# Normalized rows split into float16 halves before they are turned, and turned by DMA: a cross-attention and mixture-of-experts kernel

## What is computed

```
x = x + attention(layernorm(x), ctx)      # 16 heads of 128, 8 key/value groups, Wq Wk Wv Wo
x = x + ffn(layernorm(x))                 # the feed-forward part:
#   shared = silu(x @ shared_gate) * (x @ shared_up) @ shared_down
#   gate: sigmoid(x @ gate_w.T) + bias, best 2 of 4 groups, best 4 of 32 experts, weights normalized
#   each expert takes at most 128 rows: silu(rows @ w1) * (rows @ w3) @ w2, weighted, added to its rows
```

## Time and profile before

| | us |
|---|---|
| median of 3 runs (1817.03 to 1822.59) | 1819.76 |
| the profiled execution | 1819.97 |
| its span | 1817.9 |
| TensorE busy in the span | 1655.7 |
| VectorE busy | 1282.2 |
| ScalarE, GpSimd busy | 704.2, 650.9 |
| mean granted clock of TensorE | 0.975 |

### The profile page before, as it was taken

One profiled execution on the slowest core, in us unless ns is written; L12 is line 12 of the kernel. 1 busy time (PEld: TensorE's weight loads), 2 busy tenths in 40 slices (PEclk: granted clock), 3 DMA queues, 4 the chain that ended last, 5 costly groups with the idle time before them and its releaser, 6 DMA issues.

```text
span 1817.9 us, 32885 instructions
## 1 busy us (share of the span) xinstructions
PE 1655.7 (91%) x11472; PEld 1101.2 (61%) x11472; DVE 1282.2 (71%) x3690; ACT 704.2 (39%) x1866; POOL 650.9 (36%) x985
## 2 busy tenths in 40 slices
PE   4889999999999999999999999999999996767774
PEld 3556666666766676767676767676767673333332
DVE  5778686767676767777677777676767576676674
ACT  4454343434343434343334333333333332344452
POOL 1222333333333333333323232424242424554553
PEclk9999999999999999999999999999999998898898
DMA  6543333323233323332323232323232328699973
GB/s 187 148 120 72 59 77 59 77 59 77 59 77 55 76 57 71 58 75 59 77 53 83 53 83 53 83 53 81 55 74 51 72 51 278 185 282 263 260 213 47
DMA packets 343779, 180.63 MB, mean 99 GB/s; under 512 B 277824, under 2 KB 314688, under 8 KB 343616
## 3 DMA queue, kind: packets, MB, share of 16 engines
q1 hardware_dynamic: 332352, 161.66, 36.4%
q0 software_dynamic: 11264, 16.87, 4.6%
HBM read 85.58 MB, written 25.85 MB: 61 GB/s over the span
## 4 chain that ended last, share of the span: by engine, by line
PE 64%; DMA 12%; DVE 12%; issue 6%; ACT 3%; POOL 2%; POOLq 0%; SPq 0%; DVEq 0%; ACTq 0%
DMA out_rows_dram<-weight_in,table 9%; PE ps_out L1267 6%; PE ps_fill L1268 6%; PE ps_fill L1269 6%; PE ps_fill L1267 6%; PE ps_out L1269 6%; PE ps_out L1268 6%; PE ps_query L1267 4%; PE ps_query L1268 4%; PE ps_query L1269 4%; DVE arena L946 3%; PE ps_score L1267 3%; PE ps_score L1268 3%; PE ps_score L1269 3%; ACT arena L664 2%
## 5 line engine op out<-in xcount | busy, mean ns | idle before, releaser
L491 POOL TENSOR_SCALAR arena<-arena,prob_scale 128x256 f16<-128x256 f32 x512 | 264.3, 532 | 662.2 <-DVE prob_scale L940 662.2
L664 ACT ACTIVATE arena<-arena,neg_max 128x256 f32<-128x256 f32 x512 | 253.9, 497 | 552.7 <-DVE neg_max L931 552.7
L1267 PE MATMUL ps_query<-xn_t,arena 128*128 128x256 f16 x1024 | 279.8, 273 | 2.6 <-issue 1.5
L1268 PE MATMUL ps_query<-xn_t,arena 128*128 128x256 f16 x1024 | 279.8, 273 | 0.0
L1269 PE MATMUL ps_query<-xn_t,arena 128*128 128x256 f16 x1024 | 279.7, 273 | 0.0
L931 DVE CUSTOM_DVE_ANT_0 arena<-ps_score,mask_add 128x256 f32<-128x256 f32 x512 | 186.6, 420 | 112.0 <-PE ps_score L1269 111.1
L946 DVE SCALAR_TENSOR_TENSOR arena<-arena,prob_scale 128x256 f16<-128x256 f32 x512 | 260.1, 547 | 3.7 <-POOL arena L491 3.7
L1267 PE MATMUL ps_out<-arena,o_t 128*128 128x512 f16 x512 | 195.3, 381 | 33.3 <-DVE o_t L951 27.4
L1269 PE MATMUL ps_out<-arena,o_t 128*128 128x512 f16 x512 | 194.8, 380 | 0.0
L1268 PE MATMUL ps_out<-arena,o_t 128*128 128x512 f16 x512 | 194.8, 380 | 0.0
L855 DVE SCALAR_TENSOR_TENSOR k_t<-ps_fill,k_t 128x256 f16<-128x256 f32 x128 | 54.3, 425 | 173.4 <-ACT k_t L604 173.4
(11 more groups left out here) (198 smaller groups left out, 3827.4 us busy)
## 6 DMA issues: line engine op xcount, KB each, us to landing
arena<-w SPq DMA_DIRECT2D x96, 512.0 KB
x_in<-x SPq DMA_DIRECT2D x16, 512.0 KB, 3.9
xn_rows<-xn SPq DMA_DIRECT2D x16, 512.0 KB, 3.7
out_rows_dram<-x SPq DMA_DIRECT2D x32, 256.0 KB
ctx_in<-ctx_t SPq DMA_DIRECT2D x16, 256.0 KB, 3.6
weight_in<-wq SPq DMA_DIRECT2D x4, 1024.0 KB, 6.4
weight_in<-wo SPq DMA_DIRECT2D x4, 1024.0 KB, 5.9
arena<-arena SPq DMA_TRANSPOSE x128
```

What stands on the lines that cost most here:

```text
L491: pool.tensor_scalar(p_rows[:, 0, c, :], probs[:, c, :], prob_scale[:, c:c + 1], 1.0, ALU.mult, ALU.mult).then_inc(norm_hi, 1)
L664: act.activation(probs[:, c, :], probs[:, c, :], ACT.Exp, bias=neg_max[:, c:c + 1], scale=-1.0, accum_out=prob_sum[:, c:c + 1]).then_inc(e ...
L1267: pe.matmul(dst, a.hi, b.hi, start=start and n == 0, stop=False)
L1268: pe.matmul(dst, a.hi, b.lo, start=False, stop=False)
```

## The change

The normalized rows are split into halves as rows. xn_high (ScalarE) and xn_rest (VectorE) read the float32 rows and write xn_half, [row, half, feature] in float16; a DMA transpose on SP's queue (turn_xn) writes both halves of 128 rows, turned, into xn_both. For xn2 it is the same with xn2_high, xn2_rest and turn_xn2. The DMA transposes have half the size of turn_probs (128 x 1024 float16), two per batch for each of the two. TensorE's transposes of these rows go, but for the last batch's xn2, which TensorE turns in float16, eight tiles per 128 rows, and ScalarE copies. The value filler of turn 1's second place moves to turn 2's second place. xn2_half goes to DRAM as pairs of float16 halves, 2048 bytes per row as before; the experts' gathers read them, TensorE turns eight float16 tiles and ScalarE copies them at once, without splitting. store_xn2 moves from turn 1 to turn 2. The float32 rows get other places (x1 and parts of weight_in), expert_h moves to hidden.

```diff
+            def turn_xn(b, t):
+                if b >= 2:
+                    sp.wait_ge(pe_query, KV * (b - 1))
+                sp.wait_ge(xn_lo, TB * b + t + 1)
+                sp.dma_start_transpose(xn_both[b % 2][:, :, :, t * P:(t + 1) * P].rearrange("p h k c -> p (h k) c"),
+                                       xn_half[:, t, :, :].rearrange("p h d -> p (h d)")).then_inc(xt_turned, 16)
+
+            def turn_xn2(z, t):
+                if z:
+                    sp.wait_ge(pe_up, FSB * z)
+                sp.wait_ge(xn2_lo, TB * z + t + 1)
+                sp.dma_start_transpose(xn2_both[:, :, :, t * P:(t + 1) * P].rearrange("p h k c -> p (h k) c"),
+                                       xn2_half[:, t, :, :].rearrange("p h d -> p (h d)")).then_inc(x2t_turned, 16)
...
             sp.dma_start(bias_row[:, :], gate_bias.broadcast_to([P, E])).then_inc(in_const, 16)
+            for t in range(TB):
+                turn_xn(0, t)
             load_weight(2)
...
                 turn_probs(i)
-                if j == 1 and b:
+                if j == 2 and b:
+                    for t in range(TB):
+                        turn_xn2(b - 1, t)
                     store_xn2(b - 1)
+                if j in (4, 5) and b + 1 < B:
+                    turn_xn(b + 1, j - 4)
...
         def first(b, j):
             a, z = b + 1, b - 1
+            if j < 2:
+                return ("value", a, j, 0) if b and a < B else None
             if b == 0:
-                return ("xt", 1, j - 4) if j in (4, 5) else None
-            if j in (0, 1):
-                return ("value", a, j, 0) if a < B else None
-            if j in (4, 5):
-                return ("xt", a, j - 4) if a < B else None
-            return {2: ("x2t", z, 0), 3: ("gate", z), 6: ("rank", z), 7: ("down", z, 0)}[j]
+                return None
+            return {3: ("gate", z), 6: ("rank", z), 7: ("down", z, 0)}.get(j)
 
         def second(b, j):
...
-            if j in (0, 1):
-                return ("value", a, j, 1) if a < B else None
-            if j == 2:
-                return ("x2t", z, 1)
-            return ("up", z, j - 3) if j < 7 else ("down", z, 1)
+            if j in (0, 2):
+                return ("value", a, j // 2, 1) if a < B else None
+            return {1: None, 7: ("down", z, 1)}[j] if j in (1, 7) else ("up", z, j - 3)
...
+            def xn2_high(z, t):
+                act.wait_ge(x1_normed, TB * z + t + 1)
                 if z:
-                    act.wait_ge(pe_up, FSB * z)
-                turned_high(ps, xn2_t, t, pe_x2t, x2t_hi, TB * z + t + 1)
+                    act.wait_ge(x2t_turned, 16 * TB * z)
+                    act.wait_ge(out_xn2, 16 * z)
+                else:
+                    act.wait_ge(out_blank, 48)
+                act.activation(xn2_half[:, t, 0, :], xn2_full[:, t, :], ACT.Copy, scale=X_S).then_inc(xn2_hi, 1)
...
+                if j in (4, 5) and b + 1 < B:
+                    xn_high(b + 1, j - 4)
...
+                if j == 1 and b and i < TURNS:
+                    for t in range(TB):
+                        xn2_high(b - 1, t)
...
+            def xn2_rest(z, t):
+                dve.wait_ge(xn2_hi, TB * z + t + 1)
+                dve.scalar_tensor_tensor(xn2_half[:, t, 1, :], xn2_full[:, t, :], X_S, xn2_half[:, t, 0, :], ALU.mult,
+                                         ALU.subtract).then_inc(xn2_lo, 1)
...
+                if j == 2 and routed:
+                    xn2_rest(z, 0)
                 if live:
                     prob_scales(i)
                     filler(first(b, j), ps_fill[1])
+                if j in (4, 5) and live and a < B:
+                    xn_rest(a, j - 4)
...
+                if j == 2 and routed:
+                    xn2_rest(z, 1)
...
-            def rows_low(e):
...
             def query(i, h):
                 b, g = divmod(i, KV)
                 if h == 0:
-                    pe.wait_ge(xt_lo, TB * (b + 1))
+                    pe.wait_ge(xt_turned, 16 * TB * (b + 1))
...
+            def x2t_ready(z):
+                if z < B - 1:
+                    pe.wait_ge(x2t_turned, 16 * TB * (z + 1))
+                else:
+                    pe.wait_ge(last_copied, TB)
 
             def gate(ps, z):
-                pe.wait_ge(x2t_lo, TB * (z + 1))
+                x2t_ready(z)
...
-                rows = rows_in[e % 3].rearrange("c (p k) -> c k p", k=KD)
-                transposes(ps_fill[e % 2], [rows[:, k, :] for k in range(KD)], pe_rows)
+                rows = rows_in[e % 3].rearrange("c (h p k) -> c h k p", h=2, k=KD)
+                for n in range(2 * KD):
+                    m = pe.transpose(ps_turn[e % 2][:, n * P:(n + 1) * P], rows[:, n // KD, n % KD, :], ident_half)
+                m.then_inc(pe_rows, 1)
...
             z = B - 1
+            pe.wait_ge(ident_halved, 1)
             pe.wait_ge(*emptied(before["end", 1]))
-            xn2_transposed(ps_fill[1], z, 0)
+            last_transposed(0)
```

More of the change, by code:

```diff
@@ L118, in build @@
         x_in = [sbuf(f"x_in{n}", [TB, D]) for n in range(2)]
-        normed = sbuf("normed", [TB, D])
-        xn_t = [split(f"xn_t{n}", [KD, T]) for n in range(2)]
+        xn_half = sbuf("xn_half", [TB, 2, D], F16)
+        xn_both = [sbuf(f"xn_both{n}", [2, KD, T], F16) for n in range(2)]
+        xn_t = [Split(both[:, 0], both[:, 1]) for both in xn_both]
         ctx_in = sbuf("ctx_in", [KC, S])
@@ L146, in build, with xn_full @@
         x1 = sbuf("x1", [TB, D])
-        xn2 = sbuf("xn2", [TB, D])
-        xn2_t = split("xn2_t", [KD, T])
+        xn2_half = sbuf("xn2_half", [TB, 2, D], F16)
+        xn2_both = sbuf("xn2_both", [2, KD, T], F16)
+        xn2_t = Split(xn2_both[:, 0], xn2_both[:, 1])
+        spare = weight_in[0][:, :].rearrange("p (n t d) -> p n t d", n=2, t=TB)
+        xn2_full = spare[:, 1]
+        def xn_full(b):
+            return x1[:, :, :] if b < 2 else spare[:, 0]
         tanh_g = sbuf("tanh_g", [T])
@@ L187, in build @@
                     for n in range(AHEAD, AHEAD + HELD)]
-        rows_in = [x_in[0][:, 0, :], x_in[0][:, 1, :], x_in[1][:, 0, :]]
-        rows_t = xn_t
+        rows_in = [rows.bitcast(F16) for rows in (x_in[0][:, 0, :], x_in[0][:, 1, :], x_in[1][:, 0, :])]
+        rows_both = [both[:, :, :, :].rearrange("p h k t -> p (h k t)")[:, 0:2 * D].rearrange(
+            "p (h k c) -> p h k c", h=2, k=KD) for both in xn_both]
+        rows_t = [Split(both[:, 0], both[:, 1]) for both in rows_both]
         table = sbuf("table", [E, 2], U32)
         slot_weight = sbuf("slot_weight", [E])
-        expert_h = normed[:, 0, 0:F]
+        expert_h = hidden[:, :]
         expert_h_t = [h_t[:, 0:FB, 0:P], h_t[:, FB:2 * FB, 0:P]]
@@ L201, in build @@
         ps_any = ps_fill + ps_score
+        ps_turn = [ps[:, :].bitcast(F16) for ps in ps_fill]
         consts = signal("consts")
@@ L756, in act_program @@
                 expert_high(0, part)
-            x2t_high(ps_fill[1], z, 0)
-            x2t_high(ps_fill[0], z, 1)
+            for t in range(TB):
+                xn2_high(z, t)
+            for t in range(TB):
+                last_copy(t)
             gate_exp_neg(ps_fill[1], z)
@@ L1208, in dve_program @@
             x1_norm(z)
-            x2t_low(ps_fill[1], z, 0)
-            x2t_low(ps_fill[0], z, 1)
+            for t in range(TB):
+                xn2_rest(z, t)
             expert_low(0, 1)
@@ L1244, in dve_program @@
                 add_shared(ps_fill[t], z, t)
-            for e in range(2):
-                rows_low(e)
             for e in range(E + 1):
@@ L1293, in key @@
                 pe.wait_ge(weight_lo, prepared["wk"])
-                pe.wait_ge(*emptied(before["key", i]))
+                if i:
+                    pe.wait_ge(*emptied(before["key", i]))
                 products(ps_fill[0][:, 0:S], [(wk_s[:, k, g * HD:(g + 1) * HD], ctx_s[b % 2][:, k, :])
@@ L1302, in value, with last_transposed @@
                                     for k in range(KC)]).then_inc(pe_value, 1)
[L1304 to L1310 removed]
+            def last_transposed(t):
+                pe.wait_ge(xn2_lo, TB * (B - 1) + t + 1)
+                for n in range(2 * KD):
+                    h, k = divmod(n, KD)
+                    m = pe.transpose(ps_turn[1 - t][:, n * P:(n + 1) * P], xn2_half[:, t, h, k * P:(k + 1) * P], ident_half)
+                m.then_inc(pe_x2t, 1)
+            def x2t_ready(z):
[3 more added lines that the diff above has]
+                    pe.wait_ge(last_copied, TB)
             def gate(ps, z):
[L1313 removed]
+                x2t_ready(z)
                 pe.wait_ge(weight_lo, prepared["gate"])
@@ L1345, in filler @@
                     return
-                pe.wait_ge(*emptied(before[use]))
+                if use in before:
+                    pe.wait_ge(*emptied(before[use]))
                 kind, *at = use
@@ L1430, in pe_program @@
             pe.wait_ge(consts, CONSTS)
-            for t in range(TB):
-                x_t(ps_fill[t], 0, t)
```

140 lines of the change are left out of this document (56 added, 84 removed).

## The result

| | before | after |
|---|---|---|
| median, us | 1821.17 (4 runs, 1817.03 to 1823.10) | 1846.45 (4 runs, 1844.45 to 1849.55) |
| ratio, 95% interval | | 1.0143 [1.0119, 1.0168] |
| the profiled execution, its span | 1819.97, 1817.9 | 1849.55, 1847.8 |
| 14 batches, start of the second to start of the last | 1299.66 | 1327.51 |

Slower by 1.4%: +25 us in the medians where +14.6 was forecast, inside the range and on the forecast side. The two profiled executions are 29.9 us of span apart (the one of after is the longest of its four). By stage, from profile to profile: start to the first scores -1.9 (24.46 to 22.53), first batch +1.1, the fourteen batches +27.9, the last batch's turns +2.2, from there to the first gather -1.1, experts +1.8.

What follows compares the result with a forecast made beforehand. TensorE was taken to bound the fifteen batches behind the first. Batches +19.6, start -2, last batch's end -1.6, first batch -0.4, experts -1 sum to +14.6 us on the base: 1834.6 us, range 1818 to 1860.

Steps and rivals of the forecast that it cites:

- Rival 1: Whole kernel: the removed TensorE time counts and the gate doesn't wait, 1789 us; chance 0.11.
- rival 2: Turn 3: halves turn nearly at copy speed, gate waits 0.5 us, total 1812 to 1818; chance 0.14, spread over 1808 to 1826.
- rival 3: DMA transposes: each set-up of 1.81 us not overlapped adds 27 us (1862), two give 1889; chance 0.17 shared with two others.
- Rival 5: DMA transposes with a strided target split into smaller packets, looking like dearer turns; chance 0.17 shared with two others.
- Turn 1: Each batch: turn keeps its length since VectorE's o_t sets it; 1.64 us become idle for TensorE.
- Turn 2: Each batch: o_t starts later because xn2_rest precedes prob_scale; +0.5 us, between +0.2 and +0.6.
- Turn 3: Each batch: gate waits for xn2's two DMA transposes queued behind that of the probabilities; +1.63 us.
- rival 4: Each batch: TensorE's clock falls behind the waits, costing 1.7 us once, 1860 us; chance 0.17 shared with two others.
- Turns 4 and 5: Each batch: TensorE is the bound, four transposes leave each turn and the DMA turns are hidden; -0.44 us each.
- Its end: End of last batch: VectorE no longer waits for TensorE's transposes and makes expert low halves earlier; -1.6 us.
- First batch: First batch: eight transposes less, but it waits mostly for weights; -0.4 us (0 to -0.9).
- experts: Expert stage: little on the chain of adds except in few experts where it runs over VectorE; -1 us (0 to -2.4).

Runs made afterwards that it cites:

- Experiment 5: Changed kernel with both low halves of xn2 made at the end of turn 1 and turned behind turn 1's probabilities: 1819.11 us, 0.9999 of the kernel before.
- experiment 3: Changed kernel with one more half-size transpose, into memory nobody reads, ahead of xn2's two and waited for by the gate: 1869.88 us.
- Experiment 4: Changed kernel with the second value filler back in turn 1 instead of turn 2: 1845.01 us.
- Experiment 1: Kernel before with only the x path changed (halves as rows, turned by DMA; xn2, gathers and fillers stay): 1812.42 us, 0.9958 of the kernel before.
- experiment 9: Kernel before with only x turned by DMA, its low halves made on VectorE behind o_t in turns 4 and 5: 1807.46 us, 0.9902.
- experiment 7: Changed kernel with 128 waits for a semaphore long reached ahead of TensorE's program, shifting its instruction fetches: 1847.34 us.
- experiment 2: Changed kernel with xn2's first low half moved on VectorE behind the probabilities' scaling in turn 2: 1844.30 us, 1.0148 of the kernel before.

## Why the prediction was right, and where it was not

- **The mechanism was right**: TensorE's turns were taken out where they bought little, and a wait at the gate, behind two transposes in SP's queue, took their place. Experiment 5 moves those two out of the way, and turn 3 is 11.69 us in every batch from 2 on. Rival 1 (no wait) and rival 2 (halves at the speed of a copy) fell with the first turn 3; rival 3 (a set-up for each) fell with experiment 3. Rival 5 (smaller packets for the strided target) fell too: the trace has packets of 256 bytes for the probabilities and for the halves.
- **Turn 1** kept its length, with 1.48 us of idle for 1.64. Right.
- **Turn 2**: +0.59 for +0.5, and for the reason given (o_t 0.6 us later). Experiment 4 shows that the filler has no part in it. The forecast had the cost of xn2_rest ahead of prob_scale, by order; it lacked that the place behind costs nearly as much, by slowing GpSimd.
- **Turn 3**: +1.61 for +1.63 in an undisturbed batch, partly by luck. The forecast let bytes queue behind bytes at 215 GB/s without a gap; the halves moved faster, and the second waited for its issue on SP. The mean over the fifteen turns 3 is +2.17, and this is the term that was mis-sized. In five of the thirteen batches 2 to 14 an instruction fetch fell at the transposes and the gate started at 5.57 to 6.23 us; in three of these the clock fell behind the wait. That is rival 4 in part: it priced the fall rightly (1.7), gave it to each batch or to none, and it came in three. Together these five turns are 9.8 us longer than five of 13.30, about what the forecast was short.
- **Turns 4 and 5**: -0.49 and -0.44 for -0.44 each, right for this kernel and for a wrong reason. "TensorE is the bound" read the busy time, not the o_t, 0.06 us ahead in turn 4; and "in the same places at the same size" left out that halves made from SBUF slow GpSimd by 0.5 us. Experiment 1 gets 0.20 and 0.34 alone, and needs experiment 9's move to get the rest.
- **Start**: -1.9 for -2. **Last batch's turns**: +2.2 for +2.1. **Its end**: -1.1 for -1.6; the kernels with this edit have 55.99 to 56.18 us from the last turn's scores to the first gather, those without 56.82 to 57.08.
- **First batch** (+1.1 for -0.4) and **experts** (+1.8 for -1): not settled. The first eight turns of kernels that are the same there took 96.9 to 100.2 us, with falls of the clock in different places.

## What to carry to other kernels

Two engines that hand over at the same moment both look busy, so read the distance from the end of the one's last instruction to the start of the other's before taking work from either: here it was 0.06 us, and the gain came only when both were relieved. An instruction of the same size can cost more when its operand moves from PSUM to SBUF, and the one that pays can be another engine (0.5 us on GpSimd, per half). A transfer on the critical path costs all that stands ahead of it in its queue, its own issue, and now and then an instruction fetch; put it a turn earlier than it is needed, or leave it out of the path. Part of a change can be worth keeping where the whole is not: the turns of x, with a turn of slack each, gave 1%; those of xn2 took it back and more.

## What the runs showed of the hardware that was not expected

- An instruction fetch of 16 KB took 0.9 to 1.8 us as one packet, and a transpose whose packets met one (batch 6 of the changed kernel) all but stopped for 0.9 us (9 to 12 GB/s).
- SP took 1.25 to 2.0 us to issue one of the transposes ahead of the gate, and the first packet came 1.17 to 1.20 us behind the start of an issue where the engines were free: of transposes issued back to back, the last stood behind a gap of about 0.3 us in most batches.
- A DMA transpose of 128 x 1024 float16 moved at 236 to 293 GB/s, one of 128 x 2048 at some 215, in the same burst. Why is open.
- The clock fell behind some waits and not behind others of the same length: a wait of 3.22 us at the gate (experiment 7, batch 2) kept 1.00, one of 1.86 us (experiment 2, batch 7) was followed by a turn at 0.89. The length of the wait alone does not decide it.
- VectorE's half of a row, with both operands in SBUF, made GpSimd's four high halves take 2.67 us instead of 2.17, in turn 2 (experiment 2) and in turns 4 and 5 (the first of the four 0.97 us instead of 0.48); with one operand in PSUM it did not.
